# At most three attention gathers in flight: GpSimd waits for the third last one before it issues the next

## What is computed

```python
def _gat(x, src, dst, W, a_src, a_dst, b):        # n = 6250, 200000 edges + n self loops, H = 4
    xw = (x @ W).reshape(n, H, FH)
    al_s = jnp.einsum('nhf,hf->nh', xw, a_src)
    al_d = jnp.einsum('nhf,hf->nh', xw, a_dst)
    e = jax.nn.leaky_relu(al_s[src] + al_d[dst], NEG_SLOPE)
    m = jax.ops.segment_max(e, dst, num_segments=n)
    ee = jnp.exp(e - m[dst])
    den = jax.ops.segment_sum(ee, dst, num_segments=n)
    alpha = ee / den[dst]
    out = jax.ops.segment_sum(alpha[:, :, None] * xw[src], dst, num_segments=n)
    return out.reshape(n, H * FH) + b
h = jax.nn.elu(_bn(_gat(x, src, dst, W1, ...), g1, beta1))
h = jax.nn.elu(_bn(_gat(h, src, dst, W2, ...), g2, beta2))
```

## Time and profile before

| | us |
|---|---|
| median of 3 runs (7104.17 to 7130.43) | 7106.29 |
| span of the profiled execution | 9134.2 |
| PE / DVE / ACT / POOL busy in it | 6058.7 / 4902.9 / 2128.7 / 3226.6 |
| first and last start of a gather (L827) in it | 2895.6 and 8855.5 |

### The profile page before, as it was taken

The page is one execution under the profiler, slowest core; times in us unless marked ns, Lnnn a source line. Parts: engine busy times, 40 slices in busy tenths (PEclk is TensorE's granted clock), DMA queues, the critical chain, the costliest instruction groups (busy, mean ns, idle before and its releaser), DMA issues.

```text
span 9134.2 us, 96786 instructions
## 1 busy us (share of the span) xinstructions
PE 6058.7 (66%) x33473; PEld 4168.5 (46%) x33473; DVE 4902.9 (54%) x15778; ACT 2128.7 (23%) x3520; POOL 3226.6 (35%) x3274
## 2 busy tenths in 40 slices
PE   7999899898882565656665556516666655556663
PEld 6999677686662233333333333313333333333332
DVE  8999568584344444444444444535444444444445
ACT  3555454456441011111111111111111111111111
POOL 1221000000005444444444444264444444444432
PEclk9999999999996677777777777657777777777776
DMA  4332767789942233333333333222333333333332
GB/s 144 128 130 120 263 229 263 238 270 236 227 91 59 67 80 80 77 76 77 81 81 81 81 81 81 61 50 74 77 75 78 81 81 81 81 81 80 80 73 78
DMA packets 1103555, 1021.75 MB, mean 112 GB/s; under 512 B 467063, under 2 KB 957709, under 8 KB 1098870
## 3 DMA queue, kind: packets, MB, share of 16 engines
q1 hardware_dynamic: 998150, 790.99, 30.4%
q0 software_dynamic: 104976, 225.47, 10.2%
HBM read 569.77 MB, written 346.75 MB: 100 GB/s over the span
## 4 chain that ended last, share of the span: by engine, by line
DVE 28%; another core or an unknown queue 28%; issue 7%; PE 7%; ACT 1%; DMA 0%; DVEq 0%; SPq 0%; ACTq 0%
DVE arena L2039 10%; PE PS L1397 4%; DVE arena L2026 4%; DVE arena L2017 4%; DVE arena L2002 1%; DVE arena L2007 1%; DVE arena L2009 1%; DVE arena L2006 1%; DVE arena L2010 1%; DVE arena L2004 1%; PE PS L1306 1%; DVE arena L2001 1%; DVE arena L2049 1%; PE PS L1384 0%
## 5 line engine op out<-in xcount | busy, mean ns | idle before, releaser
L827 POOL DMA_INDIRECT arena<-table,arena x2944 | 2796.1, 950 | 2829.6 <-PE PS L1384 1960.3
L1397 PE MATMUL PS<-X,arena 128*128 128x396 bf16 x5952 | 1664.7, 409 | 1677.6 <-issue 1676.7
L1397 PEld LDWEIGHTS PS<-X,arena 128*128 128x128 bf16 x5952 | 647.4, 111 | 2618.4 <-issue 2400.7
L2049 DVE TENSOR_REDUCE arena<-PS 128x132 f32<-128x396 f32 x192 | 108.9, 567 | 2851.1 <-remote 2811.3
L1030 ACT ACTIVATE arena<-PS 128x396 f32<-128x396 f32 (+1 forms) x1078 | 528.4, 490 | 3836.2 <-PE PS L1384 3814.5
L1174 PE MATMUL PS<-count_pieces,node_halves 128*128 128x512 f32 (+1 forms) x4704 | 1086.1, 388 | 71.0 <-DVE count_pieces L1777 36.4
L2039 DVE TENSOR_SCALAR arena<-shift 128x128 bf16<-128x128 bf16 x9408 | 995.4, 187 | 176.5 <-issue 173.1
L1174 PEld LDWEIGHTS PS<-count_pieces,node_halves 128*128 128x128 f32 x4704 | 858.7, 189 | 242.5 <-issue 37.5
L1384 PE MATMUL PS<-arena 128*128 128x132 f32 x6272 | 823.1, 285 | 2.9 <-DVE arena L2026 2.6
L1113 PE MATMUL PS<-arena 128*128 128x49 bf16 x7936 | 803.3, 278 | 25.0 <-DVE arena L1615 22.6
L1113 PEld LDWEIGHTS PS<-arena 128*128 128x128 bf16 x7936 | 775.9, 150 | 55.6 <-issue 46.3
(11 more groups left out here) (372 smaller groups left out, 4952.7 us busy)
## 6 DMA issues: line engine op xcount, KB each, us to landing
arena<-counts SPq DMA_DIRECT2D x315, 896.0 KB, 4.7
segment_sums<-arena SPq DMA_DIRECT2D x96, 2176.0 KB
counts<-arena SPq DMA_DIRECT2D x31, 3136.0 KB, 9.4
arena<-table,arena POOLq DMA_INDIRECT x2944
vec<-edge_rows SPq DMA_DIRECT2D x192, 64.0 KB
arena<-counts SPq DMA_DIRECT2D x21, 448.0 KB, 3.3
table<-arena SPq DMA_DIRECT2D x2, 3332.0 KB
arena<-table SPq DMA_DIRECT2D x2, 3332.0 KB
```

The lines of the kernel that those rows point to most:

```text
L827: g_.indirect_dma_start(out=ring[n % RING][:, i, :], out_offset=None, in_=table_d[j][:, :], in_offset=bass.IndirectOffsetOnAxis(ap=other[: ...
L1397: last = t_.matmul(PS[:, 6 + t, 0:SPLIT * SW], spots[t][:, b, :], parts_of(b).rearrange("p t f -> p (t f)"), start=(b == 0), stop=(b == NB ...
```

## The change

In front of each gather, x being its number counted through both layers, GpSimd now waits until gather x - 3 has landed. The gathers raise three semaphores in turn (x % 3) in place of the one of their ring slot, and `turn_scores` waits for all three at the count that covers every gather up to the end of its batch. The ring, the order of the work on all engines, all transfers and all arithmetic stay.

```diff
     PICK = 2
+    FLYING = 3
...
-        def rows_through(n):
+        def gathers_before(n):
 
-            return sum(gathered(x % BATCHES) for x in range(n % RING, n + 1, RING))
+            return sum(gathered(x % BATCHES) for x in range(n))
...
                     for i in range(gathered(k)):
                         t = BT * k + i
+                        x = gathers_before(n) + i
+                        need(pool, f"rows_in_{x % FLYING}", 16 * (x // FLYING))
                         g_.indirect_dma_start(out=ring[n % RING][:, i, :], out_offset=None, in_=table_d[j][:, :],
                                               in_offset=bass.IndirectOffsetOnAxis(ap=other[:, t:t + 1], axis=0))\
-                          .then_inc(s[f"rows_in_{n % RING}"], 16)
+                          .then_inc(s[f"rows_in_{x % FLYING}"], 16)
...
             def turn_scores(n):
-                pe.wait_ge(s[f"rows_in_{n % RING}"], 16 * rows_through(n))
+                for q in range(FLYING):
+                    pe.wait_ge(s[f"rows_in_{q}"], 16 * ((gathers_before(n + 1) + FLYING - 1 - q) // FLYING))
```

## The result

The changed kernel takes 7559.19 us (median of 4 runs, 7553.85 to 7571.81) against 7107.01 us before (4 runs, 7104.17 to 7130.43): 452 us more, a ratio of 1.0635 with a 95% interval of 1.0618 to 1.0652. The forecast was 7397 us in a range of 7190 to 7620. The direction is right and so is most of the mechanism; the forecast loss of 291 us is 0.64 of the measured one.

The account below looks back on a forecast made before the run. The prediction took GpSimd's issue of gathers to bound the timed runs. Met waits and quiet landings cost 0; 94 stores at 3.1 us of stall add 291 us to 7106.3, giving 7397 us, range 7190 to 7620.

Parts of the forecast that it names:

- The bound: In the timed runs GpSimd's issue of gathers, one per 1.248 us, is the critical path; its sum gives 7082 us.
- The wait as an instruction: GpSimd's added wait in front of each gather costs nothing when already met: 0 us.
- The quiet landing: Away from the store a gather releases a waiting engine after 2.6 us, within the 3.74 us allowed: 0 us.
- The first stall: Beside SP's store, the third gather behind one caught by it waits for that one's landing: 3.1 us a store.
- The first stall is the whole one: The two gathers behind the stalled one find their predecessors landed in time, so no further wait under the store.
- B: The cycle's second gather in the earlier profile, started at 4107.06, caught by the store, landing after 6.3 us.
- rival 2: The stall repeats under the store, as later gathers issued singly may need 6.3 us again: 7700 us, chance 0.13.
- 94 stores: The stores of the first 47 batches of each layer meet gathers: 94 x 3.1 = 291 us.
- The profile after: Signs expected: span near 9130 us if TensorE crawls again, one 3 us table wait a batch, gaps elsewhere 0.30 us.
- Rival 1: No difference, 7106 us: gathers take turns with the store on the DMA engines and land in time; chance 0.13.
- Rival 3: Faster: a less disturbed store ends sooner within the TensorE, VectorE and ScalarE chain: down to 7038 us, chance 0.04.
- Rival 4: In timed runs the store silences q0 for only 2 to 3 us: 7200 to 7275 us, chance 0.12.

Follow-up runs that it names:

- The repeat: The kernel before, run and profiled once more without an edit: 7075.25 us, ratio 0.9998 to before.
- the removed gather: The kernel before with 29 gathers in place of 30 in every batch from a layer's fourth on: 7066.6 us against 7168.24, ratio 0.9861.

## Why the prediction was right, and where it was off

*The bound.* Right, and read against the page: the sum from the pace of GpSimd (7082 us), held against the timed runs, told that the waits of the profile were not those of the timed execution. The repeat and the removed gather show it.

*The wait as an instruction, 0.* Right (six in flight: 1.0014). *The quiet landing, 0.* Right; 2.7 us, not 2.6.

*The first stall, 3.1 us.* Right in size: 2.8 us in the store shown, and the longest wait of a store is 2.9 us in the mean of the 94 (1.7 to 3.8). Its place was about one gather off: the forecast had the waiting gather at 12 or 13 of the batch, counted from 0, and most waits of over 1 us stand at 13 and 14.

*"The first stall is the whole one."* This is the step that failed, and the term of the sum that was mis-sized: 3.1 us a store against 452 / 94 = 4.8 us. It put what follows the first stall at nothing, and that measured 1.8 us a store. I took the landings of the two gathers behind B, 1.3 and 1.0 us apart, from an execution in which both had been issued over 6 us before their packets moved (4108.31 and 4109.56) and were served one behind the other. After the change such gathers are issued one by one into the same traffic; that this is the reason fits what follows, but no run isolates it. The one started at 4028.49 released its follower only at 4036.15, 7.7 us later and 2.4 us after the first release, and the one of 4033.77 took 5.4 us (to 4039.21). So two more waits of 1.1 and 0.6 us followed. This is rival 2, in a milder form than I priced it: 1.7 us in this store, 1.8 in the mean, and not 3.2. Its condition stood in the prediction (queued in the trace, one by one after); I should have given it to the forecast itself. That 7559 us lies inside the range of 7190 to 7620 is owed to the room that the range left for rival 2, not to the forecast's own sum.

*94 stores.* Right: from the third batch of a layer on each has 3.8 to 7.3 us of waits, the first two at most 2.6.

*The profile after.* The span near 9130 us was named for the case that the crawl came again; it didn't, and the span was 7560. The signs at the gathers came: waits for the table's DMA, gaps of 0.30 us at most other gathers. More than one wait under a store was the sign given for rival 2, and it came too. *Rival 1* (no difference, by the rule of the Trainium skill, "DMA: Bandwidth & Descriptors", section "Queues, rings and completion order", that an engine takes turns between queues) fell, since the loss is there; but the silence of q0 is not the same beside every store. In the store shown no turn came to q0 in 3.5 us. At 4242.0 to 4244.5 of the same profile, beside another store, q0 did move the 32 packets of a gather, a few at a time over 2.5 us, with far less than half of the engines:

```profile
q1 hardware_dynamic: 1334, 0.73, 103.1%
q0 software_dynamic: 32, 0.07, 7.1%
```

Of the rule the trace so agrees with the turns in such a store, not with the latency that I had worked out from it: the gather started at 4239.63 released its follower only at 4245.09. *Rival 3* (faster) had no ground, since TensorE's chain has 9 us of slack. *Rival 4*, a shorter silence in the timed runs, holds for some stores and not for most. Read in quarters of a microsecond beside 40 stores of layer one in each profile, the longest silence of q0 is 4.0 to 4.25 us in the profile with the crawl, 1.25 to 4.5 us with a median of 3.75 in the repeat of before, and 1.25 to 4.5 us with a median of 3.5 in the changed kernel. In the repeat, for example, 4045.25 to 4049.5, all queues:

```profile
q1 hardware_dynamic: 2305, 1.25, 122.1%
```

So the silence of the earlier trace rows belongs to the kernel and not to the crawl. Where it was shorter the batch lost no less than 3.8 us even so.

## What to carry to other kernels

Test a profiled execution whose span is far from the timed runs before believing its waits: add up the path from the paces of the engines and see which sum gives the timed number. A limit on transfers in flight has to cover the landing time in the worst traffic of the loop, not in quiet: here 2.7 us in quiet and 5.4 to 7.7 us beside the 2.2 MB store shown (up to 8.8 us over the whole profile), so three at 1.25 us cost 6.4%, five 1.4%, and six nothing that can be measured. And landing times read from a backlog need not hold for transfers that will be issued singly: here they were too short by 1.8 us a store.

## What the runs showed of the hardware that I had not expected

Beside most stores of 4096 rows on the hardware queue the software queue got no packet for 3 to 4.5 us, in 31 of 40 stores of the repeat of before and in 24 of 40 of the changed kernel; beside the others it got a few at a time, or the pause was shorter.

On some chips a few gathers held GpSimd far longer than 0.94 us. With six in flight, the timeline of GpSimd and VectorE:

```profile
3294.11 5.09 DVE L2051 TENSOR_SCALAR arena<-shift 128x128 bf16<-128x128 bf16 x49
3294.58 4.75 POOL L838 DMA_INDIRECT arena<-table,arena  x1 [0.30 <-issue]
...
3299.58 5.11 DVE L2051 TENSOR_SCALAR arena<-shift 128x128 bf16<-128x128 bf16 x49
3299.63 6.36 POOL L838 DMA_INDIRECT arena<-table,arena  x1 [0.30 <-issue]
```

The first gather begins 0.5 us into a run of 49 short VectorE operations on bf16 and ends 0.1 us after that run; the second begins at the start of the next run and ends 1.3 us after it. The Trainium skill ("SBUF — State Buffer", section "SBUF: two separate sides") describes a lock of the port that GpSimd and VectorE share, by which GpSimd can't write descriptors while a VectorE operation holds it. The two rows fit it only in part, since the page speaks of one operation and here GpSimd is held through 49. Most batches show nothing of it: with six in flight 762 gathers started within such a run, 18 of them took over 3 us and 710 less than 1.15 us. When it happens is open. The four kernels profiled on the first chip have 17 to 32 gathers of over 3 us each, two in flight on another chip has 8, the other eight profiles none. On the first chip these gathers, with the others that took long, add some 100 us of GpSimd's time beyond the repeat of before, which is about what the kernel before takes longer there (7168 against 7080 us).

The crawl of TensorE, a matmul every 0.64 us with TensorE busy for 9.1 of the 24.5 us and VectorE idle for 30 us behind it, appeared in one profiled execution out of thirteen, and what it was stays open.
